# Two stacked deformable convolutions on one core: products on quarters of the array, and a new order of all engines' work

## What is computed

```python
x = x + L0(_gn(x)); x = x + L1(_gn(x))
# in a layer, per image:
offset = conv3x3(x, w_off) + b_off             # 18 channels (layer 1: 27, the last 9 give a mask)
py, px = base + tap + offset                   # a sampling point per tap and pixel
val = bilinear(x, py, px)                      # four corners, zero outside; layer 1: times sigmoid(mask)
out = einsum("bckhw,ock->bohw", val, w)        # 9 taps x 64 channels to 64 channels
# layer 1 then: normalise out over the whole image, gamma, beta, relu
```

## Time and profile before

| | |
|---|---|
| profiled execution | 170.41 us, span 168.6 us |
| median of 3 runs | 170.42 us |
| PE busy | 148.6 us |
| DVE, ACT, POOL busy | 104.9, 105.8, 68.0 us |
| granted TensorE clock | full in all but the last slice of 40 |
| first y spread (head ends) | 16.6 us |
| last weighted sum ends | 160.6 us |

### The profile page before, as it was taken

The page is one execution under the profiler, slowest core; times in us unless marked ns, Lnnn a source line. Parts: engine busy times, 40 slices in busy tenths (PEclk is TensorE's granted clock), DMA queues, the critical chain, the costliest instruction groups (busy, mean ns, idle before and its releaser), DMA issues.

```text
span 168.6 us, 4694 instructions
## 1 busy us (share of the span) xinstructions
PE 148.6 (88%) x1640; PEld 112.4 (67%) x1640; DVE 104.9 (62%) x248; ACT 105.8 (63%) x243; POOL 68.0 (40%) x131
## 2 busy tenths in 40 slices
PE   7999977999998989997888999998788988979920
PEld 2466634699897766774666876774666867969910
DVE  0526668987675564369986675359975667753133
ACT  3014678889768465379777575379787657864201
POOL 8601355354454434235154434235154425541011
PEclk9999999999999999999999999999999999999996
DMA  5998315200000001520000001520000000020002
GB/s 196 286 251 202 96 34 148 66 2 4 0 6 0 6 2 45 146 60 0 0 4 0 0 8 44 146 61 2 0 6 0 0 10 0 2 70 4 4 6 70
DMA packets 12757, 8.38 MB, mean 50 GB/s; under 512 B 3052, under 2 KB 11820, under 8 KB 12728
## 3 DMA queue, kind: packets, MB, share of 16 engines
q1 hardware_dynamic: 12440, 7.73, 16.9%
q10 hardware_dynamic: 288, 0.27, 0.5%
HBM read 3.31 MB, written 0.59 MB: 23 GB/s over the span
## 4 chain that ended last, share of the span: by engine, by line
PE 72%; DVE 12%; issue 9%; ACT 4%; POOL 1%; POOLq 0%; DVEq 0%; ACTq 0%
PE vb L986 18%; PE ob L1006 18%; PE ob L907 11%; PE ring L943 9%; PE ring L951 8%; DVE s L765 5%; PE vb L1081 3%; ACT xa L575 2%; PE ring L895 2%; DVE msk L718 2%; PE ring L926 2%; DVE pos L711 1%; DVE ytent L757 1%; PE ring L885 1%; ACT off L526 1%
## 5 line engine op out<-in xcount | busy, mean ns | idle before, releaser
L487 POOL TENSOR_SCALAR xa<-xa 125x384 f32<-125x384 f32 x108 | 57.5, 538 | 70.1 <-ACT xa L575 69.5
L765 DVE SCALAR_TENSOR_TENSOR s<-xa,ring 125x384 f32<-125x384 f32 x108 | 58.3, 551 | 32.9 <-PE ring L943 28.8
L575 ACT ACTIVATE xa<-ring 125x384 f32<-125x384 f32 x108 | 51.4, 488 | 17.8 <-PE ring L951 17.0
L1006 PE MATMUL ob<-val,w_d 128*64 128x192 f32 x432 | 42.6, 326 | 0.0
L951 PE MATMUL ring<-pos,soon 68*64 68x384 f16 x216 | 37.5, 329 | 3.8 <-DVE s L765 3.1
L943 PE MATMUL ring<-ytent,soon 128*64 128x384 f16 x216 | 37.4, 328 | 3.1 <-DVE ytent L757 1.3
L986 PE MATMUL vb<-s,shifted 125*64 125x216 f32 (+2 forms) x376 | 34.9, 305 | 0.9 <-DVE s L765 0.9
L1006 PEld LDWEIGHTS ob<-val,w_d 128*64 128x64 f32 x432 | 33.7, 136 | 2.5 <-issue 0.4
L986 PEld LDWEIGHTS vb<-s,shifted 125*64 125x64 f32 x376 | 24.5, 136 | 5.0 <-ACT xa L575 1.3
L598 ACT ACTIVATE val<-vb 128x432 f32<-128x432 f32 x33 | 17.5, 530 | 7.4 <-PE vb L986 6.0
L951 PEld LDWEIGHTS ring<-pos,soon 68*64 68x64 f16 x216 | 14.3, 109 | 9.8 <-issue 3.7
(11 more groups left out here) (77 smaller groups left out, 113.4 us busy)
## 6 DMA issues: line engine op xcount, KB each, us to landing
shifted<-blk SPq DMA_DIRECT2D x8, 200.0 KB
shifted<-blk SPq DMA_DIRECT2D x8, 150.0 KB
shifted<-blk SPq DMA_DIRECT2D x8, 100.0 KB
soon<-c_soon SPq DMA_DIRECT2D x1, 640.0 KB, 7.3
x_l<-x SPq DMA_DIRECT2D x2, 288.0 KB, 4.4
w_o<-w_off SPq DMA_DIRECT2D x2, 288.0 KB, 4.4
w_d<-w_def SPq DMA_DIRECT2D x4, 144.0 KB, 4.2
late<-c_late SPq DMA_DIRECT2D x1, 576.0 KB, 7.2
```

The source lines that it names most:

```text
L487: nc.gpsimd.tensor_scalar(v, v, 1.0, 0.0, ALU.min, ALU.max).then_inc(xu_ready, 1)
L575: nc.scalar.activation(xa[:, n % XA_BUFS, :], bank("x", n)[0:SPAN, 0:2 * UPX], ACT.Abs).then_inc(act_took, 1)
L765: nc.vector.scalar_tensor_tensor(out=s[u % 2][:, k // 3:k // 3 + 2 * THIRD, W * k:W * (k + 1)], in0=xa[:, n % XA_BUFS, :].rearrange("q (r ...
L1006: last = mm(sums[64 * i:64 * i + 64, 0:UPX], w_d[l][:, t, 64 * i:64 * i + 64], val[u % 2][:, t // 3:t // 3 + THIRD, W * t:W * (t + 1)], st ...
```

## The change

PE's instructions for the convolution, the weighted sums and the spreads are given smaller parts of the 128 x 128 array.

- `weighted`: per tap four products (image i, half h of the unit's pixels) with 64 rows and 64 columns instead of two with 128 rows; half 1 goes to bank 1 of ob with the images swapped. w_d is no longer block-diagonal (64 columns, no memset); evacuations `sums_out` and `residual` take three pieces.
- `conv`: per tap eight products (image i, quarter q of the image) with 64 rows and 32 columns instead of two with 128 rows and 64 columns; one job for all nine taps, in two banks of the ring; `offsets` reads it in two pieces, and the splits go by quarters of 6 image rows.
- `row_spread`: the row tents of even taps lie on lanes 0 to 63, of odd taps on 64 to 127, and each tap's product reads its 64 lanes. pos has 60 lanes instead of 68, the mask tile 59 instead of 91.
- `windows`: eight half-chunk jobs a unit instead of four (ten instead of five in the last); the same instructions.
- The final normalisation's two small products use the ring. The tables of hours are new, and so are the heads.

```diff
-OFF_LANES = 68
+OFF_LANES = 60
-MLO = 64
+MLO = 32
-YLO = 64
-YROWS = 2 * YLO
+YLO = 32
+YROWS = 128
+def tent_lane(k, part):
+    return 64 * (k % 2) + YLO * part + ROWS * (k // 2)
+QUARTERS = 4
+QROWS = H // QUARTERS
+QPX = QROWS * W
...
 UNIT = {
-    "x": {"PE": -26, "ACT": -26, "POOL": -22}, "s": {"PE": -22, "DVE": -22}, "windows": {"PE": (-1, 2, 4, 6)},
-    "values": {"ACT": (0, 2, 4, 6)}, "weighted": {"PE": (10, 10, 11, 11, 12, 13, 13, 13, 14)},
-    "sums": {"ACT": 14, "DVE": 19}, "summed": {"DVE": 20},
+    "x": {"PE": -26, "ACT": -26, "POOL": -23}, "s": {"PE": -22, "DVE": -22},
+    "windows": {"PE": (-1, 0, 0, 1, 5, 5, 6, 6)}, "values": {"ACT": (0, 2, 6, 6)},
+    "weighted": {"PE": (10, 10, 11, 11, 11, 12, 13, 13, 13)}, "sums": {"ACT": 13, "DVE": 18}, "summed": {"DVE": 21},
 }
...
 LAST_UNIT = {
-    "windows": {"PE": (-11, -10, -8, -3, -2)}, "values": {"ACT": (-10, -9, -7, -2, -1)},
-    "weighted": {"PE": (-2, -2, -2, -1, -1, -1, 2, 2, 2)},
+    "windows": {"PE": (-12, -11, -10, -10, -9, -4, -3, -3, -3, -2)}, "values": {"ACT": (-12, -11, -9, 0, 1)},
+    "weighted": {"PE": (0, 0, 0, 0, 1, 1, 4, 4, 4)},
 }
 LAYER = {
-    "aggr": {"DVE": 0}, "norm": {"PE": 2, "DVE": 0, "POOL": 3}, "normed": {"DVE": 3},
-    "xt": {"PE": (6, 7), "ACT": (6, 7)}, "conv": {"PE": (7, 8, 9, 9, 11, 13, 18, 18, 19)}, "offsets": {"ACT": 18},
-    "parts": {"DVE": 19}, "split": {"ACT": (24, 26, 26, 30), "DVE": (20, 20, 22, 23)}, "sigmoid": {"ACT": 18},
+    "aggr": {"DVE": 0}, "norm": {"PE": 3, "DVE": 0, "POOL": 3}, "normed": {"DVE": 2},
+    "xt": {"PE": (6, 7), "ACT": (6, 7)}, "conv": {"PE": 13, "ACT": 12}, "parts": {"DVE": 12},
+    "split": {"ACT": (18, 20, 21, 31), "DVE": (19, 20, 21, 22)}, "sigmoid": {"ACT": 17},
...
-HEAD_PE = [("idle", 11), ("norm", 0), ("idle", 3), ("idle quarters", 3), ("idle", 2), ("xt", (0, 0)), ("xt", (0, 1))] + [("conv", (0, k)) for k in range(5)] \
-    + [("norm", 1)] + [("conv", (0, k)) for k in range(5, TAPS)] + [("conv", (1, k)) for k in range(5)] + [("y", (0, 0))]
-HEAD_ACT = [("xt", (0, 0)), ("xt", (0, 1)), ("offsets", 0)] \
+HEAD_PE = [("idle", 11), ("norm", 0), ("idle", 8), ("xt", (0, 0)), ("xt", (0, 1)),
+           ("conv", 0), ("norm", 1), ("y", (0, 0))]
+HEAD_ACT = [("xt", (0, 0)), ("xt", (0, 1)), ("conv", 0)] \
...
-            sp.wait_ge(cleared, 7)
             for l in range(LAYERS):
                 for i in range(2):
-                    sp.dma_start(w_d[l][64 * i:64 * i + 64, :, 64 * i:64 * i + 64], w_def[l]).then_inc(wd_here[l], 16)
+                    sp.dma_start(w_d[l][C * i:C * i + C, :, :], w_def[l]).then_inc(wd_here[l], 16)
...
+                for i in range(2):
+                    wait_full(act, "conv", (m, i))
+                    nc.scalar.activation(off[:, QPX * i:QPX * (i + 1)], bank("conv", (m, i))[:, 0:QPX], ACT.Identity, bias=b_off[l])\
+                        .then_inc(act_took, 1)
...
-                nc.scalar.activation(y[:, p, UPX * j:UPX * (j + 1)], sums[:, 0:UPX], ACT.Identity, bias=b_def[l])\
-                    .then_inc(sums_taken, 1)
+                for b, there, own, h in SUMS:
+                    nc.scalar.activation(y[own, p, half_rows(j, h)], ob[there, b, 0:UPX // 2], ACT.Identity, bias=b_def[l][there, :])\
+                        .then_inc(sums_taken, 1)
...
+                for t in range(TAPS):
+                    for i in range(2):
+                        for q in range(QUARTERS):
+                            own = slice(C * i, C * i + C)
+                            last = mm(bank("conv", (m, i))[32 * q:32 * q + 32, 0:QPX], w_o[l][own, t, :],
+                                      pixels(rows_from(m, own, QROWS * q + t // 3, t % 3, QROWS), QROWS),
+                                      start=t == 0, stop=t == TAPS - 1)
...
             def row_spread(n):
                 u, k = divmod(n, TAPS)
+                half = slice(64 * (k % 2), 64 * (k % 2) + 64)
                 for d in range(2):
-                    last = mm(bank("s", n)[64 * d:64 * d + 64, 0:2 * UPX], sel[:, k, 64 * d:64 * d + 64],
-                              ytent[u % 2][:, :, :], start=True, stop=True)
+                    last = mm(bank("s", n)[64 * d:64 * d + 64, 0:2 * UPX], sel[half, k, 64 * d:64 * d + 64],
+                              ytent[u % 2][half, :, :], start=True, stop=True)
...
-                for i in range(2):
-                    last = mm(sums[64 * i:64 * i + 64, 0:UPX], w_d[l][:, t, 64 * i:64 * i + 64],
-                              val[u % 2][:, t // 3:t // 3 + THIRD, W * t:W * (t + 1)],
-                              start=t == 0, stop=t == TAPS - 1)
+                for h in range(2):
+                    for i in range(2):
+                        own, to = slice(C * i, C * i + C), C * (i ^ h)
+                        last = mm(ob[to:to + C, h, 0:UPX // 2], w_d[l][own, t, :],
+                                  val[u % 2][own, t // 3 + THIRD // 2 * h:t // 3 + THIRD // 2 * (h + 1), W * t:W * (t + 1)],
+                                  start=t == 0, stop=t == TAPS - 1)
```

220 lines of the change are left out of this document (98 added, 122 removed).

## The result

The changed kernel takes 177.53 us, median of four runs (175.16 to 179.56). The kernel before, in the same session, takes 170.68 (170.38 to 171.55). The ratio is 1.031, 95% interval 1.019 to 1.044: ratios here compare fast runs alone (those within 1.5% of the fastest of their kernel), while medians and ranges take in all runs. The profiled execution took 177.2 us at a span of 175.1, against 170.41 and 168.6 before. The forecast was 153.2, in a range of 147 to 162, with 0.06 for slower.

The account below looks back on a forecast made before the run. PE's own work was taken to bound the kernel. PE would save 24.4 us; stretches (-2.4, -5.2, -4.5, -3.0), head (-1.2) and tail (-1.0) together gave -17.3 from 170.41, so 153.2 us, range 147 to 162.

Parts of the forecast that it names:

- I take 12.5%: Last three stretches of the body: PE idle 12.5% of the time, so they change by -5.2, -4.5 and -3.0 us.
- inside the range: Head: the clock may fall in PE's new idle time; the convolution behind it would take 2.3 us more.
- Weighted sums: A tap takes 0.17 us against 0.33, saving 17.3 us of PE work in 12 units.
- Rival B: Quarters of a weighted sum do not all run at once; PE gains 7.1 us, time 163; chance 0.09.
- Convolution: Eight products run at once, a tap takes 0.25 us against 2 x 0.243; 36 taps save 8.5 us.
- Spreads: 4 of 9 s in a unit can run beside an x, saving 7.9 us of PE work.
- rival A: Spreads do not overlap; costs 7.9 us on PE, 7.5 at the end, time 161; chance 0.12.
- Switches: PE changes array shape 102 times against 28, at 0.125 us each: 9.3 us more PE work.
- The first stretch's -2.4: Units 0 to 3: ACT is at 21.8 us already, 86% of the time 25.3, so the gain is 2.4 us.
- Conv(1) moves to after x(0,3): Head and first samples: stage 1's convolution moves, leaving PE idle from 12 to 15.4 us.
- Head -1.2: Head: the first y starts near 15.4 us rather than 16.62, saving 1.2 us.
- Rival C: Every tap and odd s: row halves never overlap in real work, the switches stay; slower, 180 us; chance 0.05.

Follow-up runs that it names:

- a6: Changed kernel's order with every spread, weighted sum and convolution product on all 128 rows; 193.73 us, ratio 1.115.
- d1: Changed kernel with ACT's absolute value, POOL's clamp and DVE's product taking only the first image, PE's work the same; 174.67 us, ratio 1.019.
- d2: Kernel before with ACT's absolute value, POOL's clamp and DVE's product taking only the first image, PE's work the same; 173.9 us, ratio 1.014.
- e2: Changed kernel with ACT's evacuation of the fourth window chunk one place later in units 0 to 9; 182.19 us, ratio 1.059.
- f1: a6 with the body hours of the kernel before; 189.11 us, ratio 1.107.
- a5: Changed kernel with the convolution's products alone on all 128 rows; 185.53 us, ratio 1.086.
- a1: Changed kernel with idle products added where PE waits in the head and between the first samples; 177.3 us, ratio 1.033.
- c1: Changed kernel with stage 1's convolution in the head and idle products in head and ramp; 175.38 us, ratio 1.025.
- b1: Changed kernel with stage 1's convolution moved into the head, before the first y spread; 180.62 us, ratio 1.036.
- e3: Changed kernel with e2's later evacuation and e1's ramp together; 182.82 us, ratio 1.065.
- e1: c1 with 11 idle products in the ramp instead of 28; 179.13 us.
- b4: Changed kernel with some column spreads repeated where PE waits, some 10 us more PE work; 188.82 us.

## Why the prediction was wrong, point by point

With the clock's 7.4 us set apart, a6 gives two sums. From a6 to the changed kernel: **-17.1 us** for the parts of the array. From the kernel before to a6: **+16.5** for order, blocks and pieces. -17.1 + 16.5 + 7.4 = +6.8, which is what the profiled executions differ by (the split is an estimate, as the clock is taken out at one rate).

Three steps failed: the way from PE's work to the time ("I take 12.5%"), the unpriced move of stage 1's convolution, and the clock as "inside the range". The prices of the products were mostly right. (The terms of the sum as printed give 153.1, and the dearest switch would have added 7.8 us, not 7; neither matters here.)

- Weighted sums: 0.17 us a tap forecast; 32 of its instructions took 0.66 us, so 0.165. The price is right. Rival B (quarters that don't run at once) is out.
- Convolution: 8.5 us forecast, eight products at once; 8.0 by the medians, and 2.15 us a block at full clock, 8.6 for four. Right, though 144 columns on 64 x 32 had no row before.
- Spreads: most pairs start within 0.007 us of each other, so rival A is out as a mechanism. The size was too large: 7.9 forecast, some 5 by the units at full clock, since the s behind such a pair mostly starts 0.19 to 0.30 us after its x instead of 0.165.
- Switches: 0.125 taken, 0.12 measured (57.89 to 58.17 above). Right, from one place.
- "I take 12.5%" for PE's idle time. This is the first failed step, 11.7 of the 24.1 us with the clock's share in it. By the busy times the share came out near it (14% in the last stretch), but busy hides most of a break; the sum took prices from start to start off a busy time, which is no measure of the same thing. By starts, breaks went from 13% of the last stretch to 25%, with ACT busy 71% of it. Busy shares of the others don't give PE's waits, as the reading of the earlier trace rows supposed: the order does, as with two evacuations ahead of one xa; d1 and d2 show that the length of ACT's and DVE's instructions counts now. The prediction had seen such a wait ("DVE starves 0.7 us there", at the group of four half chunks) and left it out of the sum; the trace has DVE idle 1.05 us in that place. Its sign for this outcome, DVE's waits on s doubled, did not come: they are 30.3 us in all, 32.9 before. PE busy near 125 us was the sign that failed: it is 141.4.
- The first stretch's -2.4, which came out as +6.6. This is the second failed step, 9.0 us. The prediction wrote "Conv(1) moves to after x(0,3): PE is idle from 12 to 15.4" and gave that idle time no price. It was the time in which stage 1's convolution had been hidden. Moved, it stands in the open at 3.6 us, and the clock falls behind the gap that it left. "Head -1.2" was nearly right as an order: y came at 17.47 instead of 15.4 in the profiled execution, because of its slow warm-up, but at 15.5 to 15.9 in the seven experiments with the same head.
- The clock: "the convolution behind it would take 2.3 us more ... It is inside the range". This is the third. The mechanism was named and its size missed: the clock fell five times in ramp and body, not once, and costs 7.4 us by estimate, part of which is in the two steps above.
- Stops of PE behind an instruction packet weren't thought of at all (below).
- Rival C had the sign (slower, 180) and not the mechanism: row halves do overlap. That the time came out slower, to which the prediction gave 0.06, confirms nothing of it.

What stays open: how the ramp's loss divides between the block and the clock, other than by the estimate above; what the two banks of the ring that a block now takes cost the x, y and s around it, since before the convolution had banks of its own and no run gives them back; and whether a convolution on quarters could be issued tap by tap (it would hold the two banks all that time, which was not tried).

## What to carry to other kernels

Where a pacing engine's work is cut (here by a sixth), cost the new order first: what filled its waits before, and which slack engine's fixed order stands ahead of the next release; the product prices were the easy half and came out right. A job that becomes one block costs twice, in the gap that it leaves and in the place where it lands. Count instructions as well as columns: the smaller products made 2483 instructions of PE's 1640. And set the idle time that a change creates against the granted clock, run by run: a kernel that was always warm may not stay so.

## What was not expected of the hardware

PE stops without waiting for any engine, in dense blocks of small products above all. After the change stage 2's convolution block shows it, and so does the start of unit 4 in e2:

```profile
76.75 1.52 PE L914 MATMUL ring<-xpad,w_o 64*32 64x144 f32 x76
78.83 0.71 PE L914 MATMUL ring<-xpad,w_o 64*32 64x144 f32 x28 [0.56 <-issue]
```

```profile
65.33 0.35 PE L961 MATMUL ring<-pos,soon 60*64 60x384 f16 x2
68.11 0.53 PE L953 MATMUL ring<-ytent,soon 64*64 64x384 f16 x2 [2.43 <-issue]
```

The trace has the times of the instruction packets of the DMA (q8 of the page, 16 KB each, 23 of them against 17). In the first case a packet runs from 76.21 to 77.39 and PE goes on at 78.83, 1.43 us after its end; in the second one from 65.56 to 66.54, and PE goes on 1.57 after it. That is the rule in all twenty traces. Between 12 and 160 us they have 27 places where more than 1 us lies between the starts of two of PE's instructions and the profile names no engine for it; in 26 of them PE goes on 1.3 to 1.7 us after the end of such a packet, where by chance two would. The kernel before has none, nor have d2 and f1.

In convolution blocks on 64 x 32 parts, which issue an instruction every 15 ns at full clock, 21 of 60 have such a stop (0.3 to 1.8 us from start to start), all at full clock and all ending 1.3 to 1.7 us after a packet. In the twelve blocks on 128 rows (a5, a6, f1), where the same 144 instructions take nearly twice as long, there is none, nor in any block at half clock. So it looks as if PE runs through its code faster than it comes; this is argued from these times, and no run was made for it alone.

The longest stops fall in unit 4. In the kernels that have the changed kernel's products and body hours the length of that unit goes with the sum of its stops behind packets: 0.9 us and 14.7 us in a1, 1.1 and 14.1 in c1, 2.0 and 16.4 in the changed kernel, 3.1 and 18.7 in b1, 3.4 and 19.7 in e3, 3.8 and 19.5 in e1, 3.9 and 20.0 in e2. From the changed kernel on in this row the clock also fell within 2 us of the end of the first stop, so that the unit lost more than the stops; in b4, with stops of 2.4 us and a full clock, it took 15.9.

Products of 64 rows on the diagonal quarters write one bank of PSUM in different partitions side by side without loss (eight instructions in 0.165 us; in the earlier trace rows, where each row half had a bank of its own, the same work took 0.17 to 0.19). And idle products hold the clock full only where there is room for them: in c1 they did, and stood in the chain of the first two units with 4.5 us themselves.
